# A recurrence's steps moved from TensorE, ScalarE and VectorE to VectorE and ScalarE alone

## The reference

```python
x = x + attn_a(layernorm(x))   # gated linear attention, 16 heads, and an MLP with gelu
x = x + moe(layernorm(x))      # router over 8 experts, the best two, 256 x 256 each
x = x + attn_b(layernorm(x))   # a tanh recurrence
x = x + moe(layernorm(x))      # the same experts again
```

```python
xB = jnp.einsum('bsd,dn->sbn', x, B)          # 16 inputs a token
def step(h, xb_t):
    h = jnp.tanh(xb_t + h @ A.T)              # h: 8 sequences x 16, A: 16 x 16
    return (h, h)
_, hs = jax.lax.scan(step, h0, xB)            # 1024 steps, strictly in order
y = jnp.einsum('sbn,nd->bsd', hs, C)
return y @ W_out.T + b_out
```

## Time and profile before

| | us |
|---|---|
| median of three runs (lowest, highest) | 1695.86 (1692.9, 1700.84) |
| span of the profiled execution, first to last instruction | 1692.7 |
| TensorE busy | 1591.6 (94%) |
| VectorE busy | 1274.3 (75%) |
| ScalarE busy | 1051.2 (62%) |
| GpSimd busy | 823.1 (49%) |
| one round in the steady part | 48.6 |

### The profile page before, as it was taken

How to read it: one execution, slowest core, us unless ns; L and a number is a source line. 1 busy time by engine, 2 the same in 40 slices (tenths; PEclk the granted TensorE clock), 3 DMA queues, 4 the chain that set the end, 5 groups by cost and what they waited for, 6 DMA issues and landing times.

```text
span 1692.7 us, 51627 instructions
## 1 busy us (share of the span) xinstructions
PE 1591.6 (94%) x16840; PEld 1324.5 (78%) x16840; DVE 1274.3 (75%) x4556; ACT 1051.2 (62%) x3851; POOL 823.1 (49%) x1294
## 2 busy tenths in 40 slices
PE   4588999999999999999999999999999999998866
PEld 3477888888888888888888888888888888887654
DVE  4566777887788778787888787887888877876544
ACT  4656666666766666666666666666666667655431
POOL 3554454554555455545454554454545545543211
PEclk7799999999999999999999999999999999999978
DMA  5211111111111111011111111111111111110000
GB/s 151 84 57 45 52 58 58 42 39 43 43 56 56 56 51 43 31 52 47 56 56 56 46 42 35 50 50 56 56 56 43 37 44 44 52 52 8 7 7 13
DMA packets 117250, 81.49 MB, mean 48 GB/s; under 512 B 42016, under 2 KB 108224, under 8 KB 117056
## 3 DMA queue, kind: packets, MB, share of 16 engines
q1 hardware_dynamic: 116208, 80.10, 15.4%
q10 hardware_dynamic: 976, 0.54, 0.1%
HBM read 47.06 MB, written 33.55 MB: 48 GB/s over the span
## 4 chain that ended last, share of the span: by engine, by line
PE 82%; DVE 6%; issue 3%; DMA 3%; ACT 2%; SPq 2%; POOL 1%; ACTq 0%; DVEq 0%; POOLq 0%
PE ps L1254 62%; PE ps L1260 4%; PE ps L1271 4%; PE ps L1285 2%; PE ps L1301 2%; PE ps L1442 2%; PE ps L1331 2%; DMA xag<-in_x 2%; PE ps L1321 2%; PE ps L1312 1%; DVE hs L858 1%; DVE att L947 1%; DVE dstate L1075 1%; PE ps L1292 1%; DMA arow<-att 1%
## 5 line engine op out<-in xcount | busy, mean ns | idle before, releaser
L1254 PE MATMUL ps<-we,yT 128*128 128x512 f32 x3072 | 824.5, 411 | 0.3 <-DVE h2Ts L953 0.3
L1254 PEld LDWEIGHTS ps<-we,yT 128*128 128x128 f32 x3072 | 546.5, 191 | 100.9 <-issue 1.1
L566 ACT ACTIVATE h_lead<-ps 48x8 fp32r<-48x8 f32 x1024 | 172.4, 168 | 443.8 <-PE ps L1271 430.3
L858 DVE SCALAR_TENSOR_TENSOR hs<-ps,cst,h_lead 48x8 fp32r<-48x8 f32 x1024 | 224.7, 219 | 223.8 <-ACT ps L567 216.1
L1271 PEld LDWEIGHTS ps<-hs,aT 128*128 128x128 f32 x1024 | 195.1, 191 | 126.4 <-DVE hs L858 99.1
L1271 PE MATMUL ps<-hs,aT 128*128 128x8 f32 x1024 | 215.9, 211 | 39.7 <-DVE hs L858 38.3
L890 DVE SCALAR_TENSOR_TENSOR stage<-ps,coef,stage 128x256 f32<-128x256 f32 x384 | 183.1, 477 | 13.8 <-POOL stage L433 5.0
L890 DVE SCALAR_TENSOR_TENSOR acc<-ps,coef,acc 128x256 f32<-128x256 f32 x384 | 181.7, 473 | 6.6 <-POOL acc L433 2.7
L518 POOL TENSOR_TENSOR orstd<-omean,mhalf 128x32 f32<-128x32 f32 x32 | 174.6, 5455 | 0.2
L567 ACT ACTIVATE ps<-ps 48x8 f32<-48x8 f32 x1024 | 162.8, 159 | 0.0
L431 POOL TENSOR_TENSOR part<-part 128x256 f32<-128x256 f32 x64 | 46.9, 732 | 204.2 <-ACT part L584 201.8
(11 more groups left out here) (184 smaller groups left out, 3200.4 us busy)
## 6 DMA issues: line engine op xcount, KB each, us to landing
arow<-att SPq DMA_DIRECT2D x32, 512.0 KB, 2.8
atx<-arow SPq DMA_DIRECT2D x128, 128.0 KB, 2.8
vrow<-vtok SPq DMA_DIRECT2D x32, 256.0 KB, 2.1
vx<-vrow SPq DMA_DIRECT2D x128, 64.0 KB, 2.0
out<-stage SPq DMA_DIRECT2D x64, 128.0 KB
xin<-in_x SPq DMA_DIRECT2D x62, 128.0 KB
xag<-in_x SPq DMA_DIRECT2D x62, 128.0 KB
stage<-in_experts SPq DMA_DIRECT2D x1, 2048.0 KB, 9.5
```

Of the source, the lines that this page charges most:

```text
L566: a.activation(h_lead[:], ps[0:NB, BANK["RB"], k * B:(k + 1) * B], ACT.Tanh)
L858: v.scalar_tensor_tensor(hs[0:NB, :, k], h_whole, keeps_rest, h_lead[:].bitcast(F32), ALU.mult, ALU.subtract).then_inc(sem("rnn_h"), 1)
L1254: ins = t.matmul(dst, left(lp, c), right(rp, c), start=(n == 1), stop=(n == 3 * chunks))
```

## The change

The recurrence's steps leave TensorE. Partition 16 b + n now holds element n of sequence b, so all 8 sequences fill the 128 partitions, and the state of one step is one column of `hs` (128 x 32 steps, float32). The matrix A is laid out once per sequence (`a_in`, turned to `a_by_out`, 128x32; a pair of sequences shares a block of 32 partitions, and the other sequence's half is zero). A step k is now:

1. VectorE, `spread_state`: a turn (transpose within blocks of 32x32) of the column k - 1, read 32 times by a broadcast, so that each partition has its pair's 32 state values in a row (`h_row`).
2. VectorE, `sum_state`, directly behind it: one instruction that multiplies `a_by_out` with `h_row` and sums the row into `sum_h` (128x1). It waits for the turn by the semaphore `rnn_row`.
3. ScalarE, `state_of`: one tanh of `sum_h` with the step's input `u` as a bias per partition, written to column k of `hs`.

```diff
-            def split_state(k, count):
-
-                dve.wait_ge(sem("rnn_tanh"), past((count - 1) * TS + k + 1))
-                if k == 0:
-                    dve.wait_ge(sem("RO"), past(count - 1))
-                v.scalar_tensor_tensor(hs[0:NB, :, k], h_whole, keeps_rest, h_lead[:].bitcast(F32), ALU.mult, ALU.subtract).then_inc(sem("rnn_h"), 1)
+            def spread_state(k, count):
+
+                dve.wait_ge(sem("rnn_tanh"), past((count - 1) * TS + k))
+                last = (k - 1) % TS
+                v.transpose(h_row[:], hs[:, last:last + 1].broadcast_to([P, PAIR])).then_inc(sem("rnn_row"), 1)
+
+            def sum_state(k, count):
+
+                dve.wait_ge(sem("rnn_row"), past((count - 1) * TS + k + 1))
+                v.tensor_tensor_reduce(a_h[:], a_by_out[:], h_row[:], 1.0, 0.0, ALU.mult, ALU.add, sum_h[:]).then_inc(sem("rnn_sum"), 1)
...
             def state_of(k, count):
 
-                act.wait_ge(sem("rnn_mm"), past((count - 1) * TS + k + 1))
-                a.activation(h_lead[:], ps[0:NB, BANK["RB"], k * B:(k + 1) * B], ACT.Tanh)
-                a.activation(h_whole, ps[0:NB, BANK["RB"], k * B:(k + 1) * B], ACT.Tanh).then_inc(sem("rnn_tanh"), 1)
+                if k == 0:
+                    act.wait_ge(sem("u"), count)
+                    act.wait_ge(sem("RO"), past(count - 1))
+                act.wait_ge(sem("rnn_sum"), past((count - 1) * TS + k + 1))
+                a.activation(hs[:, k:k + 1], sum_h[:], ACT.Tanh, bias=u[:, k:k + 1]).then_inc(sem("rnn_tanh"), 1)
+
+            def keep_inputs(count):
+
+                act.wait_ge(sem("RB"), count)
+                act.wait_ge(sem("rnn_tanh"), past((count - 1) * TS))
+                a.activation(u[:], inputs, ACT.Copy).then_inc(sem("u"), 1)
```

- On TensorE every `step(k, ...)` is taken out; the projection and the readout change their form, in float32:

```diff
-            def recur(k):
-
-                return t.matmul(ps[0:NP, BANK["RB"], k * B:(k + 1) * B], aT[:],
-                                hs[:, :, (k - 1) % TS], start=False, stop=True, skip_group_check=True)
...
+            def project_inputs():
+
+                for c in range(KC):
+                    for half in range(2):
+                        for pair in range(B // 2):
+                            b = 2 * pair + half
+                            ins = t.matmul(ps[PAIR * pair:PAIR * (pair + 1), RB, 0:TS], bin_[:, c, (1 - half) * N:(3 - half) * N],
+                                           yrT[:, c, b * TS:(b + 1) * TS], start=(c == 0 and half == 0), stop=(c == KC - 1 and half == 1),
+                                           skip_group_check=True)
+                return ins
+
+            def read_out():
+
+                for b in (0, 2, 4, 6, 1, 3, 5, 7):
+                    r = slice(b // 2 * PAIR, (b // 2 + 1) * PAIR)
+                    ins = t.matmul(ps[b % BQ * TS:(b % BQ + 1) * TS, RO + b // BQ, 0:D], hs[r, :], cw[r, b % 2, :], start=True, stop=True)
+                return ins
```

- On VectorE `spread_state(k + 1)` and `sum_state(k + 1)` stand where `split_state(k)` stood. There are two exceptions: the two splits 13 and 14 stood side by side and now one step (14) stands there, and a step (16) is put in between the rest of `h2Ts` and the next expert sum. Step 24 is the last instruction of the body, step 25 the first of the next:

```diff
                 if live(it, 6):
-                    split_state(24, c6)
+                    spread_state(25, c6)
+                    sum_state(25, c6)
...
                 if live(it, 5):
-                    split_state(23, c5)
+                    spread_state(24, c5)
+                    sum_state(24, c5)
```

- On ScalarE the places of `state_of` stay. `keep_inputs` (a copy of 128x32) is added ahead of step 0, and the copy of `m1.acc` into `x2b` goes to GpSimd, which adds the output bias in the same instruction, in front of its `start_acc(m1, 0)`:

```diff
+                if live(it, 5):
+                    target = value(pool, c5)
+                    pool.wait_ge(sem("x3"), past(c5 - 1))
+                    pool.wait_ge(sem("pads_zero"), 1)
+                    pool.wait_ge(sem("mv_r"), target)
+                    g.tensor_tensor(x2b[:], m1.acc[:], bout[:].unsqueeze(1).broadcast_to([P, TILES, D]), ALU.add).then_inc(sem("x2b"), 1)
```

More of the change, by code:

```diff
@@ L89, in constants @@
     c[:, C_RESET:C_RESET + TOK] = (np.arange(TOK)[None] % TS) != 0
[L90 to L93, removed]
+    for half in range(2):
+        c[:, C_PART + half] = (p // N) % 2 == half
     return c
@@ L118, in build @@
         reset = cst[:, C_RESET:C_RESET + TOK]
-        keeps_rest, lead_sign, whole_sign = (cst[0:NB, C_PART + n:C_PART + n + 1] for n in range(3))
+        of_half = [cst[:, C_PART + half:C_PART + half + 1] for half in range(2)]
         stage = sb("stage", [P, KC * E * D])
@@ L652, in body @@
                     state_of(3, c6)
-                    act.wait_ge(sem("x3"), past(c6 - 1))
-                    act.wait_ge(sem("mv_r"), c6)
-                    a.activation(x2b[:], m1.acc[:], ACT.Copy).then_inc(sem("x2b"), 1)
                     state_of(4, c6)
@@ L1031, in body @@
                     dve.wait_ge(sem("x2b"), c6)
-                    v.tensor_tensor(m2.x[:].rearrange("p i d -> p (i d)"), ps[:, BANK["RO"], :], x2b[:].rearrange("p i d -> p (i d)"), ALU.add).then_inc(sem("x3"), 1)
+                    v.tensor_tensor(m2.x[:], recurrent, x2b[:], ALU.add).then_inc(sem("x3"), 1)
                 if live(it, 5):
-                    split_state(0, c5)
+                    spread_state(1, c5)
+                    sum_state(1, c5)
                 if live(it, 1):
@@ L1267, in moe @@
                 return product(ps[:, bank, :], lambda p, c: m.yT[:, p, c, i * P:(i + 1) * P], right, KC)
-            def recur(k):
-                return t.matmul(ps[0:NP, BANK["RB"], k * B:(k + 1) * B], aT[:],
-                                hs[:, :, (k - 1) % TS], start=False, stop=True, skip_group_check=True)
-            def step(k, count):
-                if k:
-                    pe.wait_ge(sem("rnn_h"), past((count - 1) * TS + k))
-                recur(k).then_inc(sem("rnn_mm"), 1)
+            def project_inputs():
+                for c in range(KC):
+                    for half in range(2):
+                        for pair in range(B // 2):
[9 more added lines that the diff above has]
+                return ins
             def logits(m, bank):
@@ L1491, in body @@
                     read_state(1)
-                if live(it, 5):
-                    step(4, c5)
                 if live(it, 2):
@@ L1584, in body @@
                 if live(it, 2):
-                    attend(1, False).then_inc(sem("O11"), 1)
-                if live(it, 5):
-                    step(15, c5)
+                    attend(1, isinstance(it, int) and it == 2).then_inc(sem("O11"), 1)
                 if live(it, 4):
```

261 lines of the change are left out of this document (110 added, 151 removed).

## The result

The changed kernel takes 1914.43 us (median of 4 runs, 1911.6 to 1915.86), the kernel before 1694.38 beside it: a ratio of 1.129 (95% interval 1.126 to 1.131), slower by 220 us. The forecast was 1865, the range 1715 to 2000. The profiled execution has a span of 1912.8 us.

The account below looks back on a forecast made before the run. TensorE bounds the kernel before, VectorE after: 35.9 other work + 13.8 steps + 2.0 contention + 3.4 waits = 55.1 us a round, 6.5 over 48.6; in 26 rounds +169, so 1692.7 + 169 + 3 = 1865 us, range 1715 to 2000.

Parts of the forecast that it names:

- the remaining work: VectorE's work outside the recurrence, gaps included: 35.9 us a round, which the change leaves as it is.
- The lock on turn and sum: Rival: GpSimd contention on VectorE of 4 us a round instead of 2, 57.1 a round, 1915 us; chance 0.10.
- Break-even: VectorE's new steps, their waits and all contention may together take 12.7 us a round (48.6 - 35.9).
- The step: VectorE's turn plus sum: 0.19 + 0.04 + 0.13 + 0.07 = 0.43 us, 13.8 a round; bounds 0.32 and 0.66.
- Contention: VectorE's sums held up by GpSimd's large data operations: 2.0 us a round, bounds 0 to 4.
- the row at 834.98: VectorE comparison in the earlier trace, 0.18 us during GpSimd's 5.44 us power; taken to show the power blocks nothing.
- the 2090 us that came with it: Total if the two-SBUF-input rule, taken literally, made VectorE's sums wait behind GpSimd's power: 8.6 us more a round.
- The waits that stay: VectorE's waits left after the change, walked gap by gap: 3.4 us a round, against 8.5 before.
- The wait at step 24: Step 24 to 25, no VectorE work between; VectorE waits for ScalarE's scalings, gelu and tanh: 1.2 us.
- The gate product's: After step 19, VectorE's gate product waits for ScalarE's table load and logarithm: 1.1 us a round.
- What was to be seen: Signs: VectorE above 90% busy, TensorE below 88% with waits on VectorE, round near 55 us, turn plus sum near 0.43.
- The two waits named: Sign: VectorE's waits at steps 24 (1.2 us) and 19 (1.1 us) still there after the change.

Follow-up runs that it names:

- e7: Changed kernel with VectorE's rounds written out and each multiply-and-sum replaced by a plain one-input sum, product with A left out: 1777.97 us (1.049).
- e1: Changed kernel with VectorE's 24 looped rounds written out one after the other instead of run as a hardware loop: 1858.28 us (1.095).
- e5: Changed kernel with VectorE's rounds written out and its turns and sums left out; ScalarE makes its tanh from the inputs alone: 1623.05 us (0.957).

## Why the prediction was right, by its own steps

The direction and the new bound were right, and the time was 49 us (2.6%) too low: 57.2 us a round against 55.1. Part of that closeness is luck. Against the sum's terms the round holds 2.3 us less for the steps, 1.3 more for blocked sums, 0.9 more for the other blocked operations, 3.3 more for waits and stalls, of which the loop's share was not foreseen at all, and 1.1 less in the remaining work, which no row assigns. The rival "The lock on turn and sum" (57.1 us, 1915) has the measured numbers, and its 4 us of contention are near the measured 4.2. But no turn was blocked (mean 200 ns), and its round comes out only since the errors in step, waits, loop and remaining work cancel (-2.3 + 3.3 - 1.1).

- **Break-even.** 12.7 us a round for steps, waits and contention was the right frame. The kernel after spends 11.5 on undisturbed steps, 3.3 on blocked sums and 6.7 on the listed waits and stalls; 57.2 less these is 35.7, against the 35.9 that I had worked out for the other work. (Inside it 2.0 us are new in the normalizations, and 1.1 fewer in the clip, the cast and the small addition of the earlier trace rows, so the two figures agree better than what they stand for.)
- **The step.** Forecast 0.43 us, measured 0.36, the lower part of its bounds. Turn 0.20 (forecast 0.19), gap 0.03 to 0.04 (0.04), sum to the next start 0.13 rather than 0.13 + 0.07: the accumulator read exists, 0.08 us in the record, but the next operation starts 0.01 us after it (1001.58 and 1001.59). This term was 2.3 us a round too dear, and it is the largest that the prediction mis-sized. The Trainium skill, page "VectorE: DVE Perf Modes", section "Two Vector instructions with no wait between them", has it right that there are two instructions; that 0.07 must therefore be paid was my step.
- **Contention.** Forecast 2.0 a round, bounds 0 to 4. The sums lost 3.3 and the normalizations a further 2.0: 5.3, or 4.2 net of what the kernel before already lost in small operations. I counted the sums only, though of the two rows I had one, the cast, was no two-input operation. These two (0.72 and 0.675 us) stood for blocking by a 0.74 us addition; a sum that starts behind a 128x512 one loses 1.04. The 5.44 us power blocked nothing, as the row at 834.98 said: in the kernel after it starts at 1007.94, and the sums at 1009.89 and 1011.69 take 0.19 us; the 2090 us that came with it didn't. My reading of the page "SBUF — State Buffer", section "Who interferes with whom", of the Trainium skill was too short. I took from it the rule for two SBUF inputs and found the long cast in agreement, but a cast has one. The same section also names `cast` and `tensor_scalar` among the operations that can contend under some conditions on their operands, and says that on this chip `tensor_reduce` never does. The trace agrees with each: the two-input sum is blocked, so are the cast and the y normalizations, which are scalar operations on one tensor (1.39 against 0.41 us), and the plain sum never is (e7). It doesn't agree for the power, which starts first and holds up nothing.
- **The waits that stay.** Forecast 3.4, measured 3.1 beside the stall (ScalarE's tanh 1.1, the start of the accumulation 0.8, the gate product 0.55, rf 0.4, ixf 0.3). That agreement is chance, since 1.24 us of the stall are such a wait; without it (e1) the waits are 4.4 (the turn's 2.35, 0.8, 0.5, 0.5, 0.3). The wait at step 24, forecast at 1.2, was right. The gate product's is half of my 1.1. What I left out are the waits for GpSimd and for the exponential ahead of `ixf`, 1.5 us a round together; rf and ixf were already part of the 8.5 us that I took from the round before.
- **What was missing.** The loop: stalls of 3.6 us a round in two places, of which 2.3 are its own (e1). The list of what each part of the change adds counted time per instruction and never the length of the body, which grew from 143 VectorE records a round to 206.
- **TensorE.** Removing its 32 step products did relieve it: it is busy 44.3 us of a round in e5, forecast 45, and 46.6 in e1, both at a granted clock of 1.00. The readout took 0.6 us (16 records, 1032.08 to 1032.67), forecast 1.5.
- **What was to be seen.** TensorE under 88% busy and waiting on VectorE: 84% of the round above (48.33 of 57.2), and its largest wait is that for a VectorE combination, 2.7 us a round. VectorE above 90%: wrong, 85% of a round. The stall is only part of the reason, since without it (e1) it is 88%: the waits keep VectorE from being full. Turn and sum near 0.43: no, 0.36. The two waits named: both there, the first inside the stall.

The waits of TensorE in the kernel after, 600 to 1400 us, its first two:

```profile
PE ps L1290 <- DVE stage L893: 38.2, 14, 2.9
PE ps L1328 <- DVE yT L956: 26.5, 14, 2.2
```

Of the 220 us, then: -72 from TensorE's lighter rounds (e5), +235 for turns and sums with their gaps, waits and blocking (e1 less e5; 80 of them go with the one-input sum of e7, most of that blocking), +56 for the loop (after less e1). The parts come from kernels of different groups and are good to a few us.

## What to carry to other kernels

A relief of the fullest engine is worth only what the other engines let it gain. Here TensorE's need fell by 4 us a round and the round fell by only 1.4 even with no steps on VectorE (e5), and for that 15 us (11.5 of steps, 3.3 of blocking) were put on an engine that had 9.4 free, 5.5 of them waits that the new chain has in part as well. Before adding small operations to an engine, count three prices, its start-to-start time, who locks it out at that place, and the length of its loop body; the last shows as "issue" at the loop's head and as packets on the instruction queue. And where an engine has waits of several kinds, removing a block of 1 us may bring 0.1, because the next late one stands right behind it.

## What the runs showed of the hardware

- A VectorE loop body that is too long takes 2.8 us from the branch to the next instruction at each return, with some five packets on the instruction queue a round (117 more over 24 rounds). With 253, 273 and 318 instructions a round it takes 0.3 us and with 413 it takes 2.8. A body with 32 custom sums takes 2.8 already at 316. The same work in straight-line code (e1, 6602 VectorE records) shows no such stall, though it has 72 packets on that queue against 28 in the kernel before.
- A 128x32 sum over two SBUF tiles that starts just behind a GpSimd addition (0.08 us) runs until that ends; so does a 128x256 normalization with one tensor input (0.03 us behind, 1.39 us long). A plain sum with one input beside the same additions keeps its 185 to 190 ns, and the turn its mean of 200. GpSimd's 5.44 us power beside the two-input sum leaves it at 0.19 us.
- Two independent 128x32 turns start 0.12 us apart; a dependent pair costs 0.23.
- TensorE's six 512-column products took 2.93 us where the granted clock was 0.50, the 1.2 GHz level, against 1.55 to 1.64 in the earlier trace rows at 2.4 GHz. It had waited 2.2 us for VectorE ahead of the router products. Over 600 to 1400 us the clock was 0.93. Little of this can reach the round's length directly: in those 800 us VectorE, which sets the pace, waited 0.2 us for TensorE. Timeline of TensorE in the kernel after, then that stretch by engine (columns as in the earlier trace rows):

```profile
1047.52 0.65 PE L1328 MATMUL ps<-yT,rw 128*32 128x256 f32 x4
1048.10 2.93 PE L1290 MATMUL ps<-we,yT 128*128 128x512 f32 x6
```

```profile
1048.10:1051.10 3.00, 3.00 (x12) 2.31 (x9) 2.67 (x7) 1.66 (x4) 1.52 (x2) 0.50 0.23 75
```
